# Two FiLM-conditioned linear-attention layers: x and h transposed by DMA, film applied token by token

## The reference

```python
def layer(x, emb, mask):                       # x: [8, 512, 512], emb: [8, 1024]
    xn = layernorm(x) * ln_w + ln_b            # eps 1e-5
    q = softmax(xn @ Wq + bq, over the features of a head)
    k = softmax(masked(xn @ Wk + bk), over the 512 tokens)
    v = masked(xn @ Wv + bv)
    att = per head: k.T @ v                    # [64, 64] or [32, 32]
    y = per head: q @ att
    scale, shift = split(silu(emb) @ W_emb + b_emb)      # one row each per sequence
    h = silu((layernorm(y) * ln2_w + ln2_b) * (1 + scale) + shift)
    return x + h @ W_out + b_out
```

## Time and profile before

| | us |
|---|---|
| median of 3 runs (lowest, highest) | 895.27 (894.33, 895.29) |
| the profiled execution | 894.88 |
| its span, first to last instruction | 893.1 |
| TensorE busy | 835.5 (94%) |
| VectorE busy | 717.4 (80%) |
| ScalarE busy | 537.0 (60%) |
| GpSimd busy | 382.5 (43%) |
| mean granted clock of TensorE | 0.982 |

### The profile page before, as it was taken

One profiled execution on the slowest core, in us unless ns is written; L12 is line 12 of the kernel. 1 busy time (PEld: TensorE's weight loads), 2 busy tenths in 40 slices (PEclk: granted clock), 3 DMA queues, 4 the chain that ended last, 5 costly groups with the idle time before them and its releaser, 6 DMA issues.

```text
span 893.1 us, 13959 instructions
## 1 busy us (share of the span) xinstructions
PE 835.5 (94%) x5245; PEld 457.8 (51%) x5245; DVE 717.4 (80%) x1510; ACT 537.0 (60%) x915; POOL 382.5 (43%) x328
## 2 busy tenths in 40 slices
PE   3677999999999999999999999999999999999967
PEld 2225454464555446455555545555454645555444
DVE  5898897898888788887868978687786978687675
ACT  4356384957757595874837467473838567473713
POOL 1053355434545543453554336455534536455402
PEclk9898999999999999999999999999999999999988
DMA  9922335442525434261644325244343324223322
GB/s 322 349 47 48 106 48 108 94 107 50 138 61 143 106 95 108 50 186 61 189 107 95 95 40 110 64 95 107 95 106 81 88 52 110 73 48 95 48 48 94
DMA packets 162419, 90.83 MB, mean 102 GB/s; under 512 B 134672, under 2 KB 134960, under 8 KB 162352
## 3 DMA queue, kind: packets, MB, share of 16 engines
q1 hardware_dynamic: 162352, 89.94, 39.7%
HBM read 39.60 MB, written 16.78 MB: 63 GB/s over the span
## 4 chain that ended last, share of the span: by engine, by line
PE 63%; DVE 14%; ACT 8%; issue 7%; POOL 4%; DMA 3%; SPq 1%; DVEq 0%; POOLq 0%
PE ring L418 53%; PE ring L451 4%; PE att_ps L418 3%; POOL sb_ht_lo L1215 2%; DVE sb_v_or_q L922 2%; DVE sb_q_max L925 2%; ACT sb_k_or_qt L1065 2%; ACT sb_kq_hi L1073 2%; ACT sb_tanh L1087 2%; ACT sb_xh_or_h L1094 1%; POOL sb_v_parts L1176 1%; DVE sb_y_stats L960 1%; DVE sb_kt_or_y L956 1%; DVE sb_w_lo L720 1%; DVE sb_tanh L907 1%
## 5 line engine op out<-in xcount | busy, mean ns | idle before, releaser
L418 PE MATMUL ring<-sb_w_hi,sb_xt_hi 128*128 128x512 f16 x512 | 195.1, 381 | 4.5 <-DVE sb_k_max L835 2.3
L418 PE MATMUL ring<-sb_w_lo,sb_xt_hi 128*128 128x512 f16 x512 | 195.1, 381 | 0.0
L418 PE MATMUL ring<-sb_w_hi,sb_xt_lo 128*128 128x512 f16 x512 | 194.9, 381 | 0.0
L1060 ACT ACTIVATE sb_kt_or_y<-sb_kt_or_y,sb_y_add,sb_y_rstd 128x512 f32<-128x512 f32 x64 | 46.9, 804 | 167.7 <-DVE sb_y_add L968 167.7
L1215 POOL TENSOR_TENSOR sb_ht_lo<-sb_xh_or_h,sb_ht_hi 128x512 f16<-128x512 f32 x60 | 68.4, 1170 | 114.4 <-ACT sb_ht_hi L1055 114.4
L418 PE MATMUL ring<-sb_xt_hi,sb_w_hi 128*128 128x512 f16 x256 | 97.8, 382 | 7.3 <-DVE sb_xt_lo L997 7.3
L418 PE MATMUL ring<-sb_xt_hi,sb_w_lo 128*128 128x512 f16 x256 | 97.8, 382 | 0.0
L418 PE MATMUL ring<-sb_xt_lo,sb_w_hi 128*128 128x512 f16 x256 | 97.8, 382 | 0.0
L418 PE MATMUL ring<-sb_w_hi,sb_ht_hi 128*128 128x512 f16 x240 | 91.0, 379 | 3.9 <-ACT sb_xh_or_h L1045 3.3
L418 PE MATMUL ring<-sb_w_hi,sb_ht_lo 128*128 128x512 f16 x240 | 91.0, 379 | 0.0
L418 PE MATMUL ring<-sb_w_lo,sb_ht_hi 128*128 128x512 f16 x240 | 91.0, 379 | 0.0
(11 more groups left out here) (186 smaller groups left out, 1757.8 us busy)
## 6 DMA issues: line engine op xcount, KB each, us to landing
out<-sb_x SPq DMA_DIRECT2D x15, 1024.0 KB, 4.9
sb_x<-out SPq DMA_DIRECT2D x8, 1024.0 KB, 5.8
sb_x<-in_x SPq DMA_DIRECT2D x7, 1024.0 KB, 6.3
sb_mask_raw<-in_mask SPq DMA_DIRECT2D x16, 256.0 KB, 5.9
sb_w_stage<-in_L_cond_Wk SPq DMA_DIRECT2D x2, 1024.0 KB, 6.2
sb_w_hi<-in_L_cond_W_emb SPq DMA_DIRECT2D x2, 1024.0 KB, 11.8
sb_w_lo<-in_L_cond_W_emb SPq DMA_DIRECT2D x2, 1024.0 KB, 12.9
sb_wemb<-in_L_cond_film_emb_W SPq DMA_DIRECT2D x2, 1024.0 KB, 6.2
```

Of the source, the lines that this page charges most:

```text
L418: last = nc.tensor.matmul(out, lhs, rhs, start=(n == 0), stop=(n == len(pairs) - 1))
L1060: nc.scalar.activation(kt_or_y[:, t, :], kt_or_y[:, t, :], ACT.Identity, bias=y_add[:, t:t + 1], scale=y_rstd[:, t:t + 1]).then_inc(yh_rea ...
```

## The change

- **x and h are transposed by DMA.** The normalised x (without weight and bias) is split into float16 parts token by token (`tok_hi`, `tok_lo`), and SyncE transposes both in two halves (`turn_x`), as tiles of `xt_parts`. The same buffers then hold the parts of h of the unit before (`high_h`, `low_h`), transposed whole by `turn_h`. TensorE's 32 transposes of a unit are gone, except for x of unit 0 and h of unit 15.
- **Film per token.** The film's scale and shift rows of all sequences are written to a table in DRAM (`turn_table`, `copy_table`, `store_table`), and SyncE broadcasts the two rows of a sequence to all partitions (`load_rows`). VectorE applies them with two passes a tile, `centre` and `affine`, both from SBUF; ScalarE makes the tanh from that, VectorE the product (`gate`).
- **Norm folded into the projections.** The weight of the first norm scales the rows of Wk, Wq, Wv (`ln_up`), its bias becomes a row added to their biases (`shift_parts`, `copy_shift`, `shift_sums`, `fold`); this is done in unit 0 for layer 0 and in units 3, 4 and 5 for layer 1, with TensorE's two parts on either side of V.
- **Statistics of x** move from VectorE to ScalarE (`x_spread`, sums by accumulator) and GpSimd (`x_mean`, `x_norm`), two units ahead. **The low part of q** moves from VectorE to GpSimd (`low_queries`), exp of q carries its factor.
- **Order.** Unit 0 and unit 15 do K, Q, V; the others K, V, Q. Unit 15 spreads O(14) around its attention and ends tile by tile (`tail`). Banks are given by hand (`BANKS`). Constants come in on ScalarE's DMA queue. The loops that were counted in ranges are all written out.

The core of the diff (a line of dots marks what is left out; `keys_beside_h`, `h_beside_keys` and the functions after them are called in this order in each unit's `step`):

```diff
     if u == UNITS:
+        return tiles_of("O", LAST)
+    if u in Q_FIRST:
+        front = tiles_of("K", u) + tiles_of("Q", u) + tiles_of("V", u)
+    else:
+        front = tiles_of("K", u) + tiles_of("V", u) + tiles_of("Q", u)
+    if u == 0:
+        return front + tiles_of("Y", u)
+    if u == LAST:
+        return front + tiles_of("O", u - 1, (0, 1)) + tiles_of("Y", u) + tiles_of("O", u - 1, (2, 3))
+    return front + tiles_of("O", u - 1) + tiles_of("Y", u)
...
+            def load_rows(u):
+                layer = layer_of(u)
+                sp.wait_ge(film_stored, 32 * (layer + 1))
+                sp.dma_start(rows_now[:], film_d[layer, u % B:u % B + 1].broadcast_to([P, 2, D])).then_inc(rows_loaded, 16)
...
+            def turn_h(u):
+                if u == 1:
+                    sp.wait_ge(v_lo_ready, 4)
+                else:
+                    sp.wait_ge(done["O"], 4 * (u - 1))
+                turn(ht_hi.rearrange("p t c m -> p (t c) m"), flat_hi, h_hi_ready, 4 * u, ht_hi_ready)
+                turn(ht_lo.rearrange("p t c m -> p (t c) m"), flat_lo, h_lo_ready, 4 * u, ht_lo_ready)
...
+            def turn_x(u):
+                for j in range(2):
+                    sp.wait_ge(done["V" if u in Q_FIRST else "Q"], 4 * u + 2 * j + 2)
+                    for out, source, ready, turned in ((xt_hi, flat_hi, xp_hi_ready, xt_hi_ready), (xt_lo, flat_lo, xp_lo_ready, xt_lo_ready)):
+                        turn(out[:, 2 * j:2 * j + 2].rearrange("p t c m -> p (t c) m"), source[:, 2 * j * D:2 * (j + 1) * D],
+                             ready, 4 * u + 2 * j + 2, turned)
+            def turn_q(u):
+                sp.wait_ge(kt_hi_ready, 16 * (u + 1))
+                sp.wait_ge(kt_lo_ready, 16 * (u + 1))
+                turn(blocks_of(qt_hi), kq_hi[:], q_hi_ready, 4 * (u + 1), qt_hi_ready)
+                if 0 < u < LAST:
+                    sp.wait_ge(xp_lo_ready, 4 * (u + 1))
...
+                turn_h(u)
+                turn_k(u)
+                if u == 1:
+                    load_x(3)
+                    sp.wait_ge(xp_lo_ready, 4)
+                    for dst, src in zip((bias_v[1], bias_q[1], bias_o[1]), bias_d[1]):
+                        load_row(dst[:], src, row_bias_loaded[1])
+                elif u < LAST - 1:
                     sp.wait_ge(out_stored, 16 * (u - 1))
                     load_x(u + 2)
+                if u > 1:
+                    sp.wait_ge(z_ready, 4 * u)
+                    if PREP <= u < PREP + 3:
+                        sp.wait_ge(shift_summed, 3 + u - PREP + 1)
+                    load_rows(u)
+                if u < LAST:
+                    turn_x(u)
+                turn_q(u)
+                if u == 1:
+                    sp.wait_ge(film_turned, 2)
...
-            def turn_x(u):
-                for i in range(C):
-                    if i == 0:
-                        pe.wait_ge(xh_ready, 4 * (u + 2))
-                    turn("XT", i, u, lambda c, t: xh_or_h[:, t, c * P:c * P + P])
...
+                pe.wait_ge(xt_hi_ready, 32 * u)
+                pe.wait_ge(xt_lo_ready, 32 * u)
+                if u == B:
+                    pe.wait_ge(w_ready[1], 1)
+                project_keys(u, with_k)
+                if PREP <= u < PREP + 3:
                     pe.wait_ge(att_ready, u)
+                    shift_parts(1, PREPARED[1][u - PREP])
+                if u == B:
+                    pe.wait_ge(w_ready[1], 2)
+                project_tokens("V", u, V_, xt_hi, xt_lo)
+                if u == 1:
+                    film_product(1, 0)
+                if PREP <= u < PREP + 3:
+                    shift_sums(1, PREPARED[1][u - PREP])
+                if u == B:
+                    pe.wait_ge(w_ready[1], 3)
+                project_tokens("Q", u, Q_, xt_hi, xt_lo)
+                if u == 1:
+                    film_product(1, 1)
+                    pe.wait_ge(w_scale_ready, prepared(0, O_))
+                if PREP <= u < PREP + 3:
...
+            def centre(unit, t):
+                dve.wait_ge(rows_loaded, 16 * (unit + 1))
+                nc.vector.scalar_tensor_tensor(out=kt_or_y[:, t, :], in0=kt_or_y[:, t, :], scalar=y_mean_var[:, t, 0:1],
+                                               in1=rows_now[:, 0, :], op0=ALU.subtract, op1=ALU.mult).then_inc(y_scaled, 1)
+            def affine(unit, t):
+                dve.wait_ge(y_scaled, 4 * unit + t + 1)
+                dve.wait_ge(y_rstd_ready, unit + 1 + (t if unit == LAST else 0))
+                nc.vector.scalar_tensor_tensor(out=kt_or_y[:, t, :], in0=kt_or_y[:, t, :], scalar=y_rstd[:, t:t + 1],
+                                               in1=rows_now[:, 1, :], op0=ALU.mult, op1=ALU.add).then_inc(z_ready, 1)
+            def gate(unit, t):
+                dve.wait_ge(tanh_ready, 4 * unit + t + 1)
+                nc.vector.scalar_tensor_tensor(out=kt_or_y[:, t, :], in0=tanh[:, t % 2, :], scalar=1.0, in1=kt_or_y[:, t, :],
...
+            def keys_beside_h(u):
+                for t in range(T):
+                    centre(u - 1, t)
+                masked_keys(u, 0)
+                affine(u - 1, 0)
+                affine(u - 1, 1)
+                masked_keys(u, 1)
+                gate(u - 1, 0)
+                affine(u - 1, 2)
+                masked_keys(u, 2)
+                gate(u - 1, 1)
+                affine(u - 1, 3)
+                masked_keys(u, 3)
+                key_shift(u)
+                gate(u - 1, 2)
...
+            def normalise(unit, tiles):
                 act.wait_ge(x_affine_ready, unit + 1)
+                if unit > 1:
+                    act.wait_ge(k_lo_ready, 4 * unit)
+                    act.wait_ge(ht_hi_ready, 16 * (unit - 1))
+                    act.wait_ge(h_lo_ready, 4 * (unit - 1))
+                for t in tiles:
+                    if t >= 2:
+                        act.wait_ge(xp_lo_ready, 4 * (unit - 1) + t - 1)
+                    nc.scalar.activation(normalised(unit, t), xt(unit, t), ACT.Identity, bias=x_add[:, t:t + 1],
                                          scale=x_rstd[:, t:t + 1]).then_inc(xh_ready, 1)
+                for t in tiles:
+                    act.wait_ge(xh_ready, 4 * unit + t + 1)
+                    nc.scalar.copy(tok_hi[:, t, :], normalised(unit, t)).then_inc(xp_hi_ready, 1)
...
+            def h_beside_keys(u):
+                tanh_of(u - 1, 0)
+                tanh_of(u - 1, 1)
+                high_h(u - 1, 0)
+                tanh_of(u - 1, 2)
+                high_h(u - 1, 1)
+                tanh_of(u - 1, 3)
+                exponent_of_keys(u, 0)
+                high_h(u - 1, 2)
+                exponent_of_keys(u, 1)
+                high_h(u - 1, 3)
+                exponent_of_keys(u, 2)
+                exponent_of_keys(u, 3)
...
+                high_values(u, (0,))
+                high_keys(u)
+                high_values(u, (1, 2, 3))
+                if u == 1:
+                    scale_and_split(0, O_)
+                    copy_film(1, 0)
+                elif PREP <= u < PREP + 3:
+                    copy_shift(1, PREPARED[1][u - PREP])
+                normalise(u + 1, (0, 1))
+                normalise(u + 1, (2, 3))
+                for t in range(T):
+                    high_queries(u, t)
+                if u == 1:
+                    copy_film(1, 1)
+                high_attention(u)
+                if u == 2:
+                    copy_table(1)
+                if PREP < u <= PREP + 4:
+                    scale_and_split(1, PREPARED[1][u - PREP - 1])
+                if u + 2 < UNITS:
+                    x_spread(u + 2)
...
+            def low_queries(u):
+                for t in range(T):
+                    pool.wait_ge(q_hi_ready, 4 * u + t + 1)
+                    nc.gpsimd.tensor_tensor(q_lo[:, t * D:t * D + D], q[:, t, :], kq_hi[:, t * D:t * D + D], ALU.subtract
+                                            ).then_inc(q_lo_ready, 1)
...
+            def x_spread(unit):
+                act.wait_ge(x_loaded[unit % XR], 16 * (unit // XR + (unit % XR > 0)))
+                for t in range(T):
+                    nc.scalar.activation(v_hi[:, t, :], xt(unit, t), ACT.Identity, accum_out=x_sum[:, t:t + 1]).then_inc(x_summed, 1)
+                act.wait_ge(x_minus_ready, unit - 1)
+                act.wait_ge(x_summed, 4 * (unit - 1))
+                for t in range(T):
+                    nc.scalar.activation(v_hi[:, t, :], xt(unit, t), ACT.Square, bias=x_minus[:, t:t + 1],
...
+                y_power(u - 1)
+                add_bias(u)
+                low_h(u - 1)
+                low_values(u)
+                if u == 1:
+                    low_weight(0, O_, o0_ready)
+                mask_for(u + 1)
+                low_x(u + 1)
+                low_queries(u)
+                low_attention(u)
+                if PREP < u <= PREP + 4:
+                    low_weight(1, PREPARED[1][u - PREP - 1], w_ready[1])
+                if u + 2 < UNITS:
```

(2 more changed lines are left out.)

1601 lines of the change are left out of this document (852 added, 749 removed).

## The result

The changed kernel takes 971.8 us (median of 4 runs, 968.58 to 972.52) against 894.8: ratio 1.0855, 95% interval 1.0827 to 1.0882. It is 77 us slower. The forecast was 915, range 857 to 932: the sign of the likeliest case was right, but the kernel grew by 77 us where 20 were forecast.

What follows compares the result with a forecast made beforehand. A second chain to Y, over VectorE, ScalarE, GpSimd and DMA and stretched by the lock, was taken as the bound. 148 + 54 + 3 x 57 + 2 x 53.5 + 7 x 52 + 69 = 913, so 915 us; range 857 to 932.

Steps and rivals of the forecast that it cites:

- A second chain takes 47.3 where TensorE takes 47.6: Kernel before, keys to Y: a chain over VectorE, ScalarE, GpSimd and DMA is nearly as long as TensorE's work.
- the sum: New kernel's chain added mark by mark: layer 1 period 52.0 against 50.4, all stretches together 913 us.
- the lock: GpSimd tensor_tensor and two-SBUF-input VectorE operations exclude each other, 1.68 a pair with the bias; k_shift at 17.5, without it 13.4.
- Rival (3): TensorE idles 3.3 before every Y; at the lower clock Y takes 1.4 more, 13 times: 933; chance 0.12 shared with (4).
- (4): Transposes collide in SyncE's queue, 1 us a unit: 928; chance 0.12 shared with Rival (3).
- keys of unit 1 at 87: Unit 0: x0 and weights ready earlier, but TensorE waits in K and Q and the film's table delays the end; before 90.55.
- Attention waits for the values (39): Last unit: Q before V sends q ahead, and attention is held until the values at 39.
- Y ends at 47: Last unit: Y done at 47, O 2 and 3 at 52.2, four tiles to 66, whole stretch 69 against 78.8.
- (1): The lock costs little, since VectorE's run of operations goes ahead of GpSimd's: 847, faster; chance 0.18.
- (2): Overlaps fall out kinder, by half: 881; chance 0.22.
- (5): The end's gain cancels the units' loss: no change; chance 0.04.
- by that rule the trace agrees: Claim that measured pair times fit the skill's rule: whichever operation starts first holds the shared read interface for its whole instruction.

Runs made afterwards that it cites:

- Runs 1 and 2: The former has its own line; the latter, against the changed kernel: GpSimd's four bias additions stay in place but add a constant, not the bias row: 939.2 us.
- run 1: Changed kernel with GpSimd's four output-bias additions moved from the start of a unit to its end, behind the low part of the attention: 923.65 us.

## Why the prediction missed

Of the 56 us between the forecast span and the measured one, units 0 and 1 make 27, units 2 to 14 make 21, the last unit 8.

**The bound.** "A second chain takes 47.3 where TensorE takes 47.6" held, and it is why 3.5 us less for TensorE gave nothing. In layer 1 the marks of the sum came out within 1.5 us, for unit 11: `k_shift` 17.5 forecast, 16.0 measured; last value 28.4, 27.7; mask ready 32.2, 31.9; first exp of q 37.0, 36.2; low part of q 43.8, 43.0; Y 49.3, 48.4. Runs 1 and 2 of the first question show the lock as its cause. Its price at `k_shift` was mis-sized. Behind a Y at full clock `k_shift` came at 14.1 in run 1 and at 16.9 in changed, behind slow Ys at 13.1 to 13.7 and at 15.9 to 16.7: the lock cost 2.8 and not 4.1 (17.5 - 13.4). A full collision cost what the sum says, 1.69 from one start to the next against 1.68. But of the four collisions in the sum (two centres, two affines) only two were full (1.0 more than alone), one cost 0.3, one centre was through before the additions began, and a gate lost 0.4. Without the lock `k_shift` came 0.7 later than the 13.4 of the sum, so the two errors partly cancelled.

**The clock was a rival and should have been a term.** Rival (3) had Y at 1.2 GHz for 1.4 us "13 times: 933", with (4) at 0.12. It came on top of the forecast, in 9 of the units 2 to 14. The run with the filled gaps gives its price. With Y at full clock, units 10 to 14 took 52.0 to 52.1 each, with Y 49.3 to 49.4 after the keys: the chain of the sum to the tenth, part of it by the luck of cancelling errors. Changed took 52.9 a unit in units 8 to 14. A slow Y lasts 1.4 to 2.4 longer, and of that about 1 a unit stays in the period (6.2 us in six units); it makes up the 6.3 missed in units 8 to 14. In units 6 and 7, where 4.3 is missing, Y lasted 2.4 longer in each; no run separates the clock's share there. The same thing made Q of units 3 to 5 longer: after 8.4 to 8.8 us of waiting the shift sums took 1.9 to 2.1 (1.0 in the run that put them late) and the Q behind them 11.2 to 12.7 instead of 10.5. The forecast had the wait (Q held until 30.6, measured 30.4 to 30.8) and neither of these: 3.2 a unit. The step that failed in all these units is the sum itself: each wait was costed as idle time alone, and the work behind it at full clock.

**Units 0 and 1, 27 of the 56 us.** The sum gave "keys of unit 1 at 87", 3.5 sooner than before, from a list of hindrances with no chain worked out. This step failed by the most. The trace shows TensorE waiting 5.9 for the peak of Wv, 4.8 for the sum of Q's bias, 6.6 for v's parts (Q first puts them last) and 3.9 for the table. Moves of order alone brought 103.1 to 89.9, so about 13 of the 16.1 missed are order, within a spread of some 3.5 us between profiles. In unit 1 (61 forecast, 72.1) the film's product and turn of layer 1, with 4.3 and 7.0 us of waiting for ScalarE's copies, queued behind W_out, normalise and the queries, were not in the sum at all; reordered, the unit took 63.8, and 60.1 with the bias additions, mask and shift sums late as well.

**The last unit, 7.9.** "Attention waits for the values (39)" was right (39.6). "Y ends at 47" was 49.9: behind the wait of 5.7 the attention itself ran at the lower clock, 4.6 us instead of 2.84. Then four tiles passed VectorE one after another, each with moments, centre, affine, gate, low part and residual. VectorE was busy in 18.8 of the 22 us from 941 to 963, where the sum had only TensorE's 2.6 a tile; that VectorE's load is what stretched the end is argued from this, no run takes it away. Q before V was forecast as a gain; V first was better.

**The rivals.** (1), the lock costs little, 847: refuted by run 1. (2), overlaps kinder by half: at `k_shift` by a third (2.8 of 4.1), at Y 0.7 us. (4), collisions: in unit 11 of changed none that delayed q, whose high part was sent 0.2 after it was ready; in unit 0 they were real (14.2 against 4.9 us), behind plain loads and not behind one another, and with the mask late they reached q (sent 1.9 after it was ready). (5) no. By the Trainium skill (SBUF — State Buffer, "Who interferes with whom") a GpSimd operation that reads SBUF, once it has started, shuts out a VectorE operation with two SBUF inputs for its whole length. With two inputs on GpSimd the runs agree in kind and not in full: an addition alone took 1.24 and a centre 0.75, 1.99 in turn, and a pair took 1.69. So "by that rule the trace agrees" in the prediction says too much (there 1.24 + 0.83 against 1.68). With one input they don't agree: the two operations that took 1.75 beside two inputs took 1.10 and 0.74 beside one, and the measurement decides.

**Open:** what holds units 3 to 5 and 7 at 51 to 54 us in the fastest kernels (in unit 3 TensorE still waits 2.2 for the late addition of the shift sums); why one Y in changed (unit 9) stayed at full clock after the same idle time; and why some Ys behind 2.3 us without work were slow (run 1) and others not.

## What to carry to other kernels

Taking work from the busiest engine pays only until the next chain of waits sets the time. To see how long that chain is, look at a unit of the kernel where the busiest engine has less to do. When work moves to VectorE with two SBUF inputs, place it where GpSimd has no two-input work, or move GpSimd's: here moving one call was worth 48 us, and 972 us became 870 by order alone, with the same work. Cost a wait of TensorE as the wait plus what may run behind it at the lower clock: here Y lasted 1.4 to 2.4 us longer behind most waits of 3.3 to 3.9 and behind some of 2.3, and about 1 us of it stayed in the unit. After an edit, check that the wait went and did not only move: the late shift sums saved 4 us a unit of a wait of 8.4 to 8.8, and the rest stood ahead of the attention.

## What the runs showed of the hardware

- Beside a two-input GpSimd addition (1.24 us alone) a two-input VectorE operation from SBUF took 1.75 us where it took 0.75 alone; beside a one-input GpSimd operation two such operations took 1.10 and 0.74.
- A pair of two-input operations took 1.69 us from one start to the next, less than the 1.99 of both in turn.
- A VectorE operation of only 128x4 elements (`k_shift`) took 1.08 us instead of 0.16 beside a two-input GpSimd operation.
- After 3.3 to 3.9 us without work TensorE's granted clock over Y was 0.50 to 0.65 in five of six units (4.3 to 5.3 us instead of 2.84) and 1.00 in one; with 14 matmuls in the gap it was 1.00 in all six and the kernel 7.7 us faster.
- Four half-size transposes held SyncE's queue for 1.23 us each, and for 6.88, 3.75, 1.23 and 2.30 behind 4 MB of plain loads in the same queue.
- A transpose of sixteen blocks held the queue 1.9 and 2.4 us in the pair of q, so the second went out that much later, and its source need not be ready before (run with the low part of q on VectorE).
